# A fused transformer kernel: more buffer places for the experts' pages, identity products in every tile of the last stage, new orders for that stage

## The reference, cut to what matters

```python
x = x + L0_attn(ln(x))           # delta rule, 4 heads
x = x + L0_xattn(ln(x), ctx)     # causal cross attention, 16 heads
x = x + L0_ffn(ln(x))            # 6 layers: windowed attention, 16 heads of 64, and a gated FFN
x = x + L1_attn(ln(x))           # causal attention, 16 heads of 8
x = x + L1_xattn(ln(x), ctx)     # gated (exponential decay) attention, 8 heads of 16
x = x + L1_ffn(ln(x))            # 16 experts, each token goes to its best 3
```

## Time and profile before

| | |
|---|---|
| median of two runs | 4082.86 us |
| the profiled execution | 4061.49 us |
| its span, first to last instruction | 4059.7 us |
| instructions of PE in the page | 58268 matmuls, 58268 weight loads |
| last stage of tiles | from about 3277 to 3930 us |
| tail of 42 pages | about 3930 to 4030 us |
| read back, add and store | 4030 to 4060 us |

### The profile page before, as it was taken

How to read it: one execution, slowest core, us unless ns; L and a number is a source line. 1 busy time by engine, 2 the same in 40 slices (tenths; PEclk the granted TensorE clock), 3 DMA queues, 4 the chain that set the end, 5 groups by cost and what they waited for, 6 DMA issues and landing times.

```text
span 4059.7 us, 143038 instructions
## 1 busy us (share of the span) xinstructions
PE 3798.1 (94%) x58268; PEld 2739.9 (67%) x58268; DVE 3285.5 (81%) x9302; ACT 3182.2 (78%) x9278; POOL 2692.5 (66%) x2319
## 2 busy tenths in 40 slices
PE   7999989999999999999999999999999978888873
PEld 5767756666676766766666766767666757667663
DVE  4666699998989999898889989898999847766642
ACT  3555579899999999999899999999998946656642
POOL 3444487887777777777777777777777714344444
PEclk9999999999999999999999999999999989977868
DMA  3000000000211111111201121111110000122246
GB/s 110 4 4 5 5 2 4 5 5 5 47 19 26 26 31 36 24 26 26 52 14 26 26 44 30 17 26 26 52 39 9 10 10 16 54 67 70 70 111 203
DMA packets 168664, 139.87 MB, mean 34 GB/s; under 512 B 37076, under 2 KB 148744, under 8 KB 167032
## 3 DMA queue, kind: packets, MB, share of 16 engines
q1 hardware_dynamic: 161384, 117.04, 12.9%
q0 software_dynamic: 6624, 13.68, 1.0%
HBM read 108.72 MB, written 57.23 MB: 41 GB/s over the span
## 4 chain that ended last, share of the span: by engine, by line
PE 71%; DVE 15%; ACT 8%; issue 4%; DMA 1%; POOL 1%; SPq 0%; DVEq 0%; another core or an unknown queue 0%; POOLq 0%; ACTq 0%
PE ps L682 55%; PE ps L686 16%; DVE BIG L1361 7%; ACT BIG L1107 5%; DVE sm L1372 3%; ACT BIG L1099 2%; DVE BIG L1369 1%; POOL sm L1887 1%; DVE sm L1361 1%; DMA zg<-WB 1%; DVE x_sb L1361 0%; DMA WB<-in_F_W 0%; DVE BIG L1503 0%; DVE sm L1543 0%; DVE WB L1365 0%
## 5 line engine op out<-in xcount | busy, mean ns | idle before, releaser
L1099 ACT ACTIVATE BIG<-ps 128x512 f32<-128x512 f32 (+5 forms) x2784 | 1450.8, 575 | 405.7 <-PE ps L686 235.4
L682 PE MATMUL ps<-WB,BIG 128*128 128x128 f32 (+2 forms) x6528 | 1682.1, 391 | 4.9 <-DVE BIG L1361 1.8
L1884 POOL TENSOR_TENSOR BIG<-BIG,sm 128x512 f32<-128x512 f32 (+1 forms) x864 | 1214.7, 1430 | 673.1 <-DVE sm L1543 305.2
L686 PEld LDWEIGHTS ps<-t_ident,BIG 128*128 128x128 f32 x5952 | 717.4, 144 | 486.2 <-issue 299.3
L1884 POOL TENSOR_TENSOR BIG<-BIG 128x512 f32<-128x512 f32 x776 | 972.8, 1280 | 87.4 <-DVE BIG L1361 72.4
L686 PE MATMUL ps<-t_ident,BIG 128*128 128x128 f32 x5952 | 914.4, 281 | 75.4 <-DVE BIG L1369 38.6
L682 PEld LDWEIGHTS ps<-WB,BIG 128*128 128x128 f32 (+1 forms) x6528 | 863.2, 192 | 174.3 <-issue 153.5
L1372 DVE TENSOR_REDUCE sm<-BIG 128x8 f32<-128x512 f32 (+5 forms) x1440 | 857.1, 623 | 6.9 <-ACT BIG L1107 5.2
L682 PEld LDWEIGHTS ps<-BIG 64*64 64x64 f32 (+2 forms) x37888 | 605.0, 128 | 321.6 <-issue 145.5
L682 PE MATMUL ps<-BIG 64*64 64x64 f32 (+4 forms) x37888 | 728.6, 222 | 62.8 <-ACT BIG L1107 18.1
L1107 ACT ACTIVATE BIG<-ps,sm 128x64 f32<-128x64 f32 (+1 forms) x3104 | 700.6, 394 | 37.7 <-DVE sm L1372 35.8
(11 more groups left out here) (152 smaller groups left out, 3557.1 us busy)
## 6 DMA issues: line engine op xcount, KB each, us to landing
xg<-in_F_empty SPq DMA_DIRECT2D x64, 520.0 KB, 8.1
WB<-in_F_W SPq DMA_DIRECT2D x111, 257.0 KB
WB<-in_Wqkv SPq DMA_DIRECT2D x6, 1536.0 KB, 7.5
WB<-xg SPq DMA_DIRECT2D x111, 65.0 KB
xg<-in_F_empty SPq DMA_DIRECT2D x6, 1040.0 KB, 7.6
BIG<-zg SPq DMA_DIRECT2D x8, 768.0 KB, 10.0
XS<-y_sb SPq DMA_DIRECT2D x96, 63.0 KB
y_sb<-in_ctx SPq DMA_DIRECT2D x16, 256.0 KB, 3.8
```

The lines of the kernel that those rows point to most:

```text
L682: return te.matmul(o, l, r, start=start, stop=stop, skip_group_check=not check)
L686: return te.transpose(o, i, ident[0:n, 0:n])
L1099: return se.activation(o, i, ACT.Copy)
L1884: return pe_.tensor_tensor(o, a, b, op)
```

## The change

Three things change.

1. Rows get 16 places and results 12; weights keep 8, which are now counted by `NFW`. Rows move from the tensor WB to unused columns of BIG. For page j SyncE waits for PE's page j - 8 (for the weights) and for the landed scatter of page j - 16 (for the rows). DVE waits for the scatter of page j - 12.
2. Four PE items `Bf` with two products each stand in every tile of the last stage, 32 tiles, besides the 15 products of tiles 0 to 8.
3. All four order strings of the last stage are new, with a SLOT of 15.538 in place of 14.030 and other BEGINs.

```diff
-NXB, NYB = 8, 4
+NFW, NXB, NYB = 8, 16, 12
 DE_ORDER = {
-    "pe": "g37 av6 X13 p04 Bh19 cs5 Bo09 J3 BT29 u4 rk7 Bo19 Bh29 G5 t4 T3 w4 Bo29 s3 gT7 BT08 xc4 ct5 b27 Bh08 om5 g4 "
-           "X36 BT18 p13",
+    "pe": "Bf04 w6 rk9 s5 X14 BT0b om7 BT1b Bf38 Bh0b xc6 J4 Bh1b BT2b p05 gT9 Bo0b g6 Bh2b p15 b29 ct7 Bo1b u5 Bo2b "
+           "X38 cs6 av7 g38 T4 Bf13 t5 G6 Bf24",
...
-    "dve": "mm4 st23 h45 s36 gg6 ix6 ag23 og6 Bo28 C4 xn23 x5 c12 st35 ag35 c02 st10 xn35 xn11 ge3 cu6 b26 md4 ab3 ag10 "
-           "m35 ti5 ls3 id5 a04 cf5 a14 oh5 a24 gs5 a34 mb5 cs3 a44 gj3 hh4 a1 s14 Bo07 v1 h24 ss1 su5 rk5 n01 r2 v14 n2 "
-           "sl5 gm5 qn1 Bo17 dm3 mx3 w2 gr5",
-    "pool": "Bz17 Bz27 gb2 id4 Bz06 d22 bo0 h53 h63 sc4",
+    "dve": "csb ra Bo2g gjb na a0c m3d a1c a2c a3c tid st18 a4c idd hhc cfd sud ag18 s1c dmb ohd mxb h2c gsd mbd wa gmd "
+           "mmb v1c st2a grd ag2a xn18 rkd ggd Cb c09 xn2a c19 h4c mdb ogd sld a8 s3d v8 ixd xc st3c gea ag3c aba Bo0f "
+           "ss8 n08 xn3c lsa b2d Bo1f qn8 cud",
+    "pool": "Bz09 bo2 h55 h65 sc6 gb3 Bz19 Bz29 d23 id5",
 }
-SLOT = {"ab": 13.426, "c": 11.263, "de": 14.030, "fb": 1.2, "fc": 3.0}
+SLOT = {"ab": 13.426, "c": 11.263, "de": 15.538, "fb": 1.2, "fc": 3.0}
-    "de": {"pe": 3221.92, "act": 3186.93, "dve": 3246.05, "pool": 3263.81},
+    "de": {"pe": 3186.91, "act": 3225.23, "dve": 3120.03, "pool": 3236.32},
...
-                            if u.at["t"] >= FROM:
+                            if u.at["t"] >= FROM and ph[1] != "f":
...
                     for j in range(u.at["first"], u.at["n"]):
+                        if j >= NFW:
+                            w.wait_ge(*FB[j - NFW].on("pe", "o"))
                         if j >= NXB:
-                            w.wait_ge(*FB[j - NXB].on("pe", "o"))
                             w.wait_ge(f"ys{(j - NXB) % NYB}", 16 * ((j - NXB) // NYB + 1))
```

More of the change, by code:

```diff
@@ L292, in build @@
         tables = WB[0:1, 532:532 + 128 * len(STEPS)].bitcast(I32)
[L293 to L297, removed]
+        FW = [WB[:, 1428 + 514 * p:1942 + 514 * p] for p in range(NFW)]
+        XB = [BIG[:, 23250 + 130 * p:23380 + 130 * p] for p in range(NXB)]
+        YB = [WB[:, 5540 + 128 * p:5668 + 128 * p] for p in range(NYB)]
+        XT = [WB[:, 7076 + 128 * p:7204 + 128 * p] for p in range(4)]
+        HID = [WB[:, 7588 + 256 * p:7844 + 256 * p] for p in range(4)]
         xg = nc.dram_tensor("xg", (XROWS, 130), F32, kind="Internal").ap()
@@ L368, in build @@
         names += ["wat0", "wat1", "wq", "wf", "out", "rt", "empty", "const", "rope", "ones", "blank", "prime", "half", "shift"]
-        names += [f"xr{i}" for i in range(3)] + [f"bw{i}" for i in range(NXB)]
+        names += [f"xr{i}" for i in range(3)] + [f"bw{i}" for i in range(NFW)]
         names += [f"ys{i}" for i in range(NYB)] + ["lists", "seen"]
@@ L622, in blocks @@
                         at = eng.value_load(tables[0:1, c:c + 1], min_val=0, max_val=XROWS - 128)
-                        eng.dma_start(XB[j % NXB], xg[bass.ds(at, 128), :]).then_inc(sems[f"bw{j % NXB}"], 16)
-                        eng.dma_start(FW[j % NXB], din["F_W"][bass.ds((at >> 12) * 128, 128), :]).then_inc(sems[f"bw{j % NXB}"], 16)
+                        eng.dma_start(XB[j % NXB], xg[bass.ds(at, 128), :]).then_inc(sems[f"bw{j % NFW}"], 16)
+                        eng.dma_start(FW[j % NFW], din["F_W"][bass.ds((at >> 12) * 128, 128), :]).then_inc(sems[f"bw{j % NFW}"], 16)
             def results():
@@ L670, in _ @@
             w.wait_ge("rt", 16)
-            for i in range(NXB):
-                w.wait_ge(f"bw{i}", 32 * len(range(i, PAGES, NXB)))
+            for i in range(NFW):
+                w.wait_ge(f"bw{i}", 32 * len(range(i, PAGES, NFW)))
         c_again = 32 if "C" in stages else 16
@@ L1075, in pe_fb @@
                     w.wait_ge(*v.on(e, m))
-                K, W = bank[u.bank[ph]], FW[j % NXB]
+                K, W = bank[u.bank[ph]], FW[j % NFW]
                 if ph == "T":
-                    w.wait_ge(f"bw{j % NXB}", 32 * (j // NXB + 1))
+                    w.wait_ge(f"bw{j % NFW}", 32 * (j // NFW + 1))
                     o = tr(K[:, 0:128], XB[j % NXB][:, 0:128])
                 elif ph == "h":
-                    w.wait_ge(f"bw{j % NXB}", 32 * (j // NXB + 1))
+                    w.wait_ge(f"bw{j % NFW}", 32 * (j // NFW + 1))
                     w.wait_ge(*u.on("act", "T"))
```

## The result

| | before | after |
|---|---|---|
| median of the runs | 4082.86 us | 4136.88 us (4130.31 and 4143.44) |
| the profiled execution | 4061.49 us | 4143.44 us |
| its span | 4059.7 us | 4141.6 us |

The ratio after to before is 1.0148, 95% interval 1.0111 to 1.0185 (the plain quotient of the two medians is 1.0132). The forecast of 4010 us, with its range up to 4066, missed on the wrong side. That is more than the medians' 54 us, since the kernel before varies (4060 to 4083 us in 19 executions on one chip) and its profiled execution is one of the quick ones.

What follows compares the result with a forecast made beforehand. It took PE's turn-taking with DVE, plus a stop and half-rate clock in page tiles, as the bound, and SyncE's loads in the tail. Terms +1.4 - 64.1 + 5 + 0 - 15.2 = -72.9 us gave 4010 us, range 3980 to 4066.

Steps and rivals of the forecast that it cites:

- The clock stays near full in page tiles: Last stage, page tiles: clock over 0.95, PE the bound; 17 x (16.9 - 20.67) = -64.1 us.
- Rival B: Page tiles: the stop at scatters stays on the path, 18.9 us a tile; 4044, or 4066 with clock falls; chance 0.23.
- Turn-taking gone: Last stage's tiles: by the new lists, PE and DVE no longer take turns around C, 4.5 us a tile.
- the bounds of 16.0 and 17.9: Tiles without pages: period limits in us a tile; 16.5 taken, twelve tiles giving +1.4 us.
- the bounds of 16.0 and 18.5: Page tiles at full clock: 16.0 us if PE never waits, 18.5 with no fills hidden; 16.9 taken.
- Eight products 2.1 us at full clock: PE, all 32 tiles: added identity products cost 2.1 us a tile, 4.2 at half clock, where PE bounds.
- C's 4093: Rival for the last stage's tiles: nothing won, clock falls as now, +1.1 us a page tile; +10 us, 4093; chance 0.13.
- D's 4169: Rival: products make PE the bound at 1.2 GHz, +4.2 us on 17 tiles, +2.1 on 12; +86, 4169; chance 0.03.
- the banks that fill items take: PE's fill items: each waits for a slightly younger item's reader, unpriced, between 0 and 1.9 us a tile.
- Depth and drain +5: End of the last stage: deeper lists and later pages leave a page or three more, +5 us (0 to +16).
- start 0: Start of the last stage: PE's earlier first item and fills taken as 0 us, ends -12 and +16.
- Places -15.2: Tail: SyncE stops waiting for landed scatters, 41 loads at 1.76 instead of 2.13 us; -15.2 us, ends 0 and -16.

Runs made afterwards that it cites:

- e8_xg_last: The changed kernel with POOL's three scatters of rows (sc) moved from ahead of gb to the end of POOL's list: 4050.33 us, ratio 0.9944.
- e3_places: The kernel before with only the places changed (16 rows, 12 results, 8 weights), old orders, no added products: 4056.09 us, ratio 0.9958.
- e1_nofill: The changed kernel without the eight identity products of every tile, orders and places as changed: 4085.82 us, ratio 1.0035.
- e9_xg_last_no_products: The changed kernel with the rows' scatters at the end of POOL's list and without the eight products a tile: 4052.48 us, ratio 0.9950.
- e10_old_xg_behind_id: Old orders, new places, no added products; on POOL's list sc moved right behind gb and id, Bz1 and Bz2 behind bo: 4192.38 us, ratio 1.0297.
- e11_xg_behind_gb: The changed kernel with its eight products and the rows' scatters (sc) moved behind gb on POOL's list: 4155.33 us, ratio 1.0207.

## Why the prediction was wrong, step by step

By ratios the change comes apart so: places 0.9958, -17 us; new orders without products 1.0035 / 0.9958 = 1.0077, +31 us; products 1.0148 / 1.0035 = 1.0113, +46 us; together +60 us. With the rows' scatters away from `u` the last two are 0.9944 / 0.9958 = 0.999, about -6 us and not clear of noise. The rows of the profiled pair give 81.9 us and not 60, for the reason named with the result.

1. **The clock stays near full in page tiles, and so in those without: the step that failed.** It was 0.78 and 0.82. The forecast took the fall to follow from PE's waits, which more work would shrink. That is so where no scatter stands near (0.92 with the products, 0.80 without), but in this change's lists another cause came first: three scatters beside `u`. Half a microsecond inside `u` was followed by 6.8 us at half rate, worth up to 3.4 us a tile. A tile without pages took 21.3 us (tiles 3 to 7) where e8_xg_last, with the scatters moved and a held clock, took 17.4. The argument that tiles without pages kept their clock rested on one execution; e3_places had 0.90 there in the same orders.
2. **Rival B had the mechanism, but the wrong price and stage.** It left the stop on the path of page tiles at 2 us and gave 4044 to 4066. I looked at the zg scatters beside av, as the earlier trace rows show them, and did not follow the rows' scatters: in the new list `sc` stands ahead of `gb`, and so beside `u`, in all 32 tiles. Moving that one item takes back 83 us.
3. **Turn-taking gone: wrong.** The lists put ct behind C, but PE still waited for that C, 15.5 us in 11 times in 3560 to 3880 (22.1 in 15 before), since a place in a list doesn't say when PE comes to it. Even at a held clock a tile without pages took 17.4 us, not the 16.5 taken; the bounds of 16.0 and 17.9 held. A page tile took 19.4 us at a clock of 0.92, against 16.9 taken; with up to 1.6 us of that for the clock (16% of the time at half rate, an estimate) it lies within the bounds of 16.0 and 18.5, near the upper one.
4. **Eight products 2.1 us at full clock: about right.** 2.6 us a tile in the old orders. That they help the clock was right with no stop near (0.92 against 0.80), and they gain nothing in all. In the changed kernel itself they cost 46 us. C's 4093 and D's 4169 stand on either side of the result, which is chance: both put most of their loss in page tiles, and 60 of the 87 us lie in the others. For the banks that fill items take the forecast had no row, and used nothing. With the products PE waits 2.3 to 2.6 us for DVE at `s` in every fourth tile (five times in 3360 to 3890), and without them, in e1_nofill and e9_xg_last_no_products, it has no such wait; whether the banks are the cause isn't shown.
5. **Depth and drain +5, start 0:** the first tile came 4.9 us later, and from the last tile to the first load of the tail it took 5.4 us more. Both lie within the ends.
6. **Places -15.2: the mechanism was right,** SyncE's wait for zg went to nothing, the loads gave 10.4 us, since with almost no wait shown (0.5 us in all) they took 1.88 us and not 1.76 in the mean; the places alone gave 17 us (8 to 25 by the interval).

What stays open: what in a scatter stops PE's narrow runs and delays DVE's start, and why the clock held in one execution of the old orders and not in another. For the first, a kernel that writes the rows with plain transfers in place of scatters would tell; it wasn't tried.

## What to carry to other kernels

Before an engine's order is changed, mark in the timeline where POOL's indirect scatters start and what runs in the 2 us behind each: runs of many small matmuls and the reader of a fresh result should stand clear. A gap of half a microsecond can cost 3 us more by the clock that falls behind it, so a forecast has to price the gap by both. A clock that is full in one execution needn't be full in the next: look at a second one before a forecast rests on it. Expect extra products at best to pay for themselves. Compare PE's waits on "issue" of two kernels stage by stage, with what PE runs there. When a scatter is moved on POOL's list, also ask what POOL item now stands behind it and who waits for that.

## What the runs showed of the hardware

- PE went on 1.69 us (after), 1.90 us (e10_old_xg_behind_id) and 1.95 us after the start of the last of POOL's scatters nearby, and DVE 1.75 us (e11_xg_behind_gb) and 1.98 us. Wide matmuls beside scatters mostly show no such gap: in e8_xg_last PE works from 3427.76 on beside the scatters of 3427.91 and 3429.18. But it isn't for narrow runs alone. In the same run a transpose waited 1.19 us, 1.22 us after the scatter of 3501.06 started:

```profile
3502.28 0.33 PE L687 MATMUL ps<-t_ident,BIG 128*128 128x128 f32 x1 [1.19 <-issue]
```

- The same 64 matmuls took 1.12 us whole, 2.2 us with one gap, 5.3 us among four scatters.
- The busy share of a stretch does not tell its clock: in 3369 to 3536 PE was busy 88% at 0.98 (e8_xg_last) and 88% at 0.90 (e3_places).
- Loads with almost no wait shown often come 1.72 us apart (4025.27 to 4026.99), yet 41 of them took 1.88 us in the mean, with single ones from 1.28 to 3.51 us apart.
